# The second norm's mean from VectorE's accumulator, its variance from ScalarE's squares

## The chip, the core and the metric

The kernel runs on one core of a Trainium2 chip. Its engines are named as in the profile: PE is TensorE (matrix products), DVE VectorE, ACT ScalarE, POOL GpSimd, SP the engine that issues the DMA transfers. Each works through its own list of instructions in order and waits on semaphores for the others. The metric is the device time of one execution in microseconds (us); lower is better.

## The reference

```python
x = x + 0.5 * ffn(_layernorm(x, ...))       # x: 2048 tokens x 512
x = x + attn(_layernorm(x, ...))            # the "second norm" is this one
x = x + 0.5 * ffn(_layernorm(x, ...))

def _layernorm(x, axis=-1, eps=1e-05):
    m = jnp.mean(x, axis=axis, keepdims=True)
    v = jnp.var(x, axis=axis, keepdims=True)
    return (x - m) / jnp.sqrt(v + eps)

def ffn(x):     # 64 experts, each a bias vector; the best 8 of the softmax count
    scores = softmax(x @ router_weight.T + router_bias)
    topk_w, topk_idx = top_k(scores, 8)
    w_dense = zeros.at[..., topk_idx].add(topk_w)
    return x * topk_w.sum() + w_dense @ expert_bias

def attn(x):    # 32 heads of q, 8 of k and v, 128 wide, chunks of 128 tokens
    dt = softplus(x @ Win.T + dt_bias); g = -dt * exp(A_log)
    y = intra-chunk (scores * decay) @ (v * dt) + inter-chunk state
    return (rmsnorm(y) * gnorm_w * silu(x @ Wg.T)) @ Wo.T
```

## The kernel before

The 2048 tokens are 16 chunks of 128 tokens (one per partition), four chunks to a block; f counts blocks, 0 to 3 for the first ffn and 4 to 7 for the last. The order of every engine's instructions is written out by hand, and between engines there are only semaphores.

The run has three parts. A prologue of some 100 us does the first ffn, the second norm and what attention needs of its first block. Then 8 groups of heads x 16 steps follow, one chunk a step, and at the end the last ffn. Only the prologue has a second norm.

For each block the prologue goes as follows. The first norm's statistics come from DVE (`dve_stats` with w = 0) and POOL turns them into 1/sqrt(variance + eps), RSTD, and -mean times it, NMR (`pool_rstd`). PE turns the chunk (`pe_turn`), ACT copies it (`act_turned`, FXT), PE makes the logits, DVE adds the bias and finds the maxima (`dve_logits`, FLG), ACT takes the exponentials (`act_exp`, FEX), DVE weighs them (`dve_choose`, `dve_weigh`), PE turns the weights (`pe_weights`), ACT copies them (`act_weights`, FWT), PE mixes the experts' biases in two PSUM banks in turn (`pe_mix`), POOL scales the residual (`pool_residual`) and DVE adds the two in ACC (`dve_mixed`, L701). That is the experts' addition. Its result is what the second norm sees: `dve_stats` with w = 1 takes its statistics, `pool_rstd` again RSTD and NMR, ACT normalises into XN (`act_normalise`, L711), PE turns XN (`pe_turn2`, L720), ACT copies the high half as bf16 (`act_turned2`, XTH, L726) and DVE subtracts for the low half (`dve_turned2`, XTL, L733). PE's turns share three PSUM banks in rotation: turn k waits until turn k - 3 has been read, so the last turn of a block waits for XTL of its first chunk.

Woven in are weights (ACT makes WH, L1120, and POOL WL), the step sizes' softplus (`dve_dt_in`, ACT's Exp at L772, then `dve_series`, L779 to L801), and the first projections `fill`, whose banks ACT exchanges by halves for the rotary embedding (`swap`, QS, L1136 and L1137), POOL multiplies by the sine, and DVE multiplies by the cosine (`times_cos`, L1610) and adds (`add_sin`, L1615). `times_cos` of an item waits for its `swap`; a `swap` waits for the `add_sin` two items before. `gate` (L1161) is a Tanh of a projected bank.

## Time and profile before

| | |
|---|---|
| time, median of 3 runs | 1639.38 us (1639.04 to 1642.29) |
| profiled execution, its own time | 1642.75 us |
| its span | 1640.9 us |
| mean granted PE clock | 0.989 |
| busy share of the span | PE 97%, DVE 83%, ACT 67%, POOL 86% |

The span is what the profiler saw, from the first instruction to the last; the time holds 1.85 us more around it. The busy shares are means over the whole run. The row of 40 equal slices shows that the first three slices are unlike the rest: PE is at 7 to 9 tenths there, and at 9 in nearly all that follow.

### The profile page before, as it was taken

The page shows a single profiled execution, that of the slowest core. Times are in us where ns is not written, and L with a number is a line of the kernel's source. Part 1 is how long each engine was busy: PE and PEld are TensorE (multiplying, and loading weights), DVE is VectorE, ACT ScalarE, POOL GpSimd, SP SyncE. Part 2 cuts the span into 40 slices and gives each one's busy share as a digit, 9 for nine tenths or more (in the row PEclk, how much of TensorE's full clock was granted, in tenths as well). Part 3 has the DMA queues.
Part 4 walks back from the last instruction along what each step waited for, and adds up shares of the span by engine and source line. Part 5 has one row for each costly group of instructions (what it writes and reads, how often), then busy time and mean ns, then how long its engine had stood idle before and what let it go on. Part 6 is the DMA issues. An engine that isn't in the chain of part 4 may idle for free.

```text
span 1640.9 us, 33589 instructions
## 1 busy us (share of the span) xinstructions
PE 1589.4 (97%) x11028; PEld 883.8 (54%) x11028; DVE 1368.9 (83%) x2945; ACT 1093.0 (67%) x2987; POOL 1411.7 (86%) x1316
## 2 busy tenths in 40 slices
PE   7898999999999999999999999999999999999986
PEld 5554555555555555555555555555555555555554
DVE  6988788888878888787878888788888878788876
ACT  4666677676766677766766667666776667666653
POOL 4767899888988899888998989888998889888974
PEclk8999999999999999999999999999999999999998
DMA  5123233232333223231332224323342224322222
GB/s 211 39 55 67 55 74 87 65 72 52 78 85 78 53 59 102 54 83 47 91 78 64 61 64 92 72 72 53 73 95 59 72 46 97 72 65 52 53 45 103
DMA packets 208012, 118.76 MB, mean 72 GB/s; under 512 B 173792, under 2 KB 174816, under 8 KB 206816
## 3 DMA queue, kind: packets, MB, share of 16 engines
q1 hardware_dynamic: 207840, 116.63, 29.7%
q8 instruction: 89, 1.46, 0.4%
q14 instruction: 83, 0.68, 0.1%
HBM read 70.19 MB, written 4.46 MB: 45 GB/s over the span
## 4 chain that ended last, share of the span: by engine, by line
PE 74%; POOL 11%; DVE 8%; issue 4%; ACT 2%; DMA 0%; ACTq 0%; POOLq 0%; DVEq 0%
PE B L325 23%; PE B L323 23%; PE B L324 23%; POOL QS L1410 2%; POOL ROWS L1423 2%; POOL RR L1456 1%; DVE WL L1696 1%; POOL PL L1445 1%; PE B L553 1%; POOL ZS L1449 1%; POOL WVF L1433 1%; POOL K L1417 1%; POOL WVL L1441 1%; POOL RM L1453 1%; DVE PF L1640 1%
## 5 line engine op out<-in xcount | busy, mean ns | idle before, releaser
L323 PE MATMUL B<-WH,XTH 128*128 128x128 bf16 (+1 forms) x992 | 269.3, 296 | 0.6 <-DVE QF L1610 0.6
L324 PE MATMUL B<-WL,XTH 128*128 128x128 bf16 (+1 forms) x992 | 269.3, 296 | 0.0
L325 PE MATMUL B<-WH,XTL 128*128 128x128 bf16 (+1 forms) x992 | 269.3, 296 | 0.0
L1410 POOL TENSOR_TENSOR QS<-QS,SIN 128x512 f32<-128x512 f32 x160 | 219.3, 1371 | 42.8 <-ACT QS L1137 42.7
L323 PE MATMUL B<-XTH,WH 128*128 128x512 bf16 x640 | 243.2, 380 | 1.0 <-DVE G L1630 1.0
L325 PE MATMUL B<-XTH,WL 128*128 128x512 bf16 x640 | 243.3, 380 | 0.0
L324 PE MATMUL B<-XTL,WH 128*128 128x512 bf16 x640 | 243.2, 380 | 0.0
L1689 DVE SCALAR_TENSOR_TENSOR YF<-B,RR,G 128x128 f32<-128x128 f32 x512 | 144.2, 344 | 113.4 <-POOL RR L1456 113.3
L1169 ACT ACTIVATE PF<-ROWS,NG 128x128 f32<-128x128 f32 x512 | 162.7, 389 | 79.1 <-POOL ROWS L1423 78.8
L1449 POOL TENSOR_TENSOR ZS<-YF,ZS 128x512 bf16<-128x512 f32 x128 | 158.0, 1235 | 64.5 <-ACT ZS L1207 64.2
L1136 ACT ACTIVATE QS<-B 64x512 f32<-64x512 f32 x160 | 94.9, 593 | 150.3 <-PE B L325 143.5
L1423 POOL TENSOR_TENSOR ROWS<-ROWS,AFTER 128x512 f32<-128x512 f32 x128 | 189.8, 1483 | 2.4 <-DMA ROWS<-rows_dram 2.4
L323 PE MATMUL B<-WH,ZT 128*128 128x512 bf16 x480 | 181.9, 379 | 0.2 <-DVE ACC L1703 0.2
L324 PE MATMUL B<-WL,ZT 128*128 128x512 bf16 x480 | 181.9, 379 | 0.0
L325 PE MATMUL B<-WH,ZT 128*128 128x512 bf16 x480 | 181.9, 379 | 0.0
L1678 DVE TENSOR_TENSOR STL<-ST,STH 128x512 bf16<-128x512 f32 x120 | 145.1, 1209 | 39.4 <-ACT STH L1189 37.6
L1445 POOL TENSOR_TENSOR PL<-PF,PH 128x512 bf16<-128x512 f32 x128 | 148.1, 1157 | 17.8 <-ACT PH L1175 17.4
L1640 DVE SCALAR_TENSOR_TENSOR PF<-B,DT,PF 128x128 f32<-128x128 f32 x512 | 143.0, 339 | 21.7 <-ACT PF L1169 20.2
L1199 ACT ACTIVATE YF<-B 128x128 f32<-128x128 f32 x512 | 134.0, 276 | 31.1 <-DVE B L1656 28.2
L1615 DVE TENSOR_TENSOR QF<-QF,QS 128x512 f32<-128x512 f32 x128 | 138.0, 1080 | 5.1 <-POOL QS L1410 4.0
L1433 POOL TENSOR_TENSOR WVF<-VF,WJ 128x512 f32<-128x512 f32 x120 | 141.8, 1181 | 0.2
L1456 POOL TENSOR_TENSOR RR<-RM,HALF 128x4 f32<-128x4 f32 x128 | 132.8, 1037 | 10.0
(209 smaller groups left out, 4320.9 us busy)
## 6 DMA issues: line engine op xcount, KB each, us to landing
ROWS<-rows_dram SPq DMA_DIRECT2D x128, 256.0 KB, 3.2
STAGE<-in_wall SPq DMA_DIRECT2D x108, 256.0 KB, 2.8
ACC<-in_x SPq DMA_DIRECT2D x3, 1024.0 KB, 10.0
out<-ACC SPq DMA_DIRECT2D x3, 1024.0 KB, 3.9
ZT<-ZS SPq DMA_TRANSPOSE x128, 3.1
ACC<-in_x SPq DMA_DIRECT2D x4, 256.0 KB, 3.6
COS<-in_cos SPq DMA_DIRECT2D x1, 1024.0 KB, 12.0
SIN<-in_sin SPq DMA_DIRECT2D x1, 1024.0 KB, 14.7
```

The costliest lines, as they stand in the source:

```text
L323: nc.tensor.matmul(out_, ah, bh, start=first, stop=False)
L324: nc.tensor.matmul(out_, ah, bl, start=False, stop=False)
L325: return nc.tensor.matmul(out_, al, bh, start=False, stop=last)
L1169: ins = nc.scalar.activation(PF[:, c], ROWS[:, n % 2, c], ACT.Exp, bias=tab(NG, g, n)[:, h:h + 1], scale=-1.0)
L1410: nc.gpsimd.tensor_tensor(QS[:, sl, :], QS[:, sl, :], SIN[:, t0:t0 + TB], ALU.mult).then_inc(sin_ready.sem, 1)
L1423: nc.gpsimd.tensor_tensor(rows, rows, AFTER[:, None, :].broadcast_to([P, G, P]), ALU.add).then_inc(rows_masked.sem, 1)
L1433: nc.gpsimd.tensor_tensor(WVF[:, :, :], VF[b % 2][:, None, s * P:(s + 1) * P].broadcast_to([P, G, P]), tab(WJ, g, n)[:, :, None].broadcast ...
L1445: nc.gpsimd.tensor_tensor(PL[:, :], PF[:, :], PH[:, :], ALU.subtract).then_inc(pl_ready.sem, 1)
L1449: nc.gpsimd.tensor_tensor(ZS[:, 1, :], YF[:, :], ZS[:, 0, :], ALU.subtract).then_inc(zl_ready.sem, 1)
L1456: nc.gpsimd.tensor_tensor(RR[:, :], RM[:, :], HALF[:, :], ALU.pow).then_inc(rr_ready.sem, 1)
L1640: ins = nc.vector.scalar_tensor_tensor(PF[:, c], B_S[:, c], dt[:, h:h + 1], PF[:, c], ALU.mult, ALU.mult)
L1678: nc.vector.tensor_tensor(STL[:, :], ST[:, :], STH[:, :], ALU.subtract).then_inc(stl_ready.sem, 1)
```

## The change

The second norm takes its statistics in another way. DVE's experts' addition writes its sum over the 512 columns as well (`accum_out`, SM). POOL makes from it -mean/sqrt(512) (`pool_mean`, two chunks at a time). ACT squares the chunk with that as bias and 1/sqrt(512) as scale, and its accumulator sums the squares, which is the variance (`act_square`, VR); the squares themselves go to memory that is free at the time and aren't used. `pool_rstd` takes SM and VR in place of the aggregate. bn_stats and bn_aggr of the second norm are gone from DVE (16 and 16 of them).

```diff
-        def dve_stats(dve, w, f, chunks=range(BLK)):
+        def dve_stats(dve, f, chunks=range(BLK)):
...
+        def pool_mean(pool, f, half):
+            pool.wait_ge(f_acc.sem, f_acc.at(f, 2 * half + 1))
+            if f >= 2:
+                pool.wait_ge(f_sq.sem, f_sq.at(f - 2, BLK - 1))
+            c = slice(2 * half, 2 * half + 2)
+            nc.gpsimd.tensor_scalar(SMB[:, f % 2, c], SM[:, f % 2, c], -float(HID) ** -1.5, None, ALU.mult).then_inc(f_mean.sem, 1)
+
+        def act_square(act, f, chunks=range(BLK)):
+            A = chunks_of(f)
+            for i in chunks:
+                act.wait_ge(f_mean.sem, f_mean.at(f, i // 2))
+                if f >= 2:
+                    act.wait_ge(f_lg.sem, f_lg.at(f, 0))
+                    act.wait_ge(f_ve[1].sem, f_ve[1].at(f - 2, 0))
+                elif f:
+                    act.wait_ge(f_tp2.sem, f_tp2.at(f - 1, i))
+                nc.scalar.activation(XN[:, i, :] if f < 2 else FIRST.XT[:, f % 2, i, :], A[:, i, :], ACT.Square, bias=SMB[:, f % 2, i:i + 1],
+                                     scale=float(HID) ** -0.5, accum_out=VR[:, f % 2, i:i + 1]).then_inc(f_sq.sem, 1)
...
+            if w:
+                pool.wait_ge(f_sq.sem, f_sq.at(f, BLK - 1))
+            else:
+                pool.wait_ge(f_mv.sem, f_mv.at(f, 0))
...
+                if f < NB:
+                    if f >= 2:
+                        dve.wait_ge(f_nmr[1].sem, f_nmr[1].at(f - 2, 0))
+                    nc.vector.scalar_tensor_tensor(A[:, i, :], mix(f, i)[:, :], e.HRC[:, f % NB, i:i + 1], A[:, i, :],
+                                                   ALU.mult, ALU.add, accum_out=SM[:, f % 2, i:i + 1]).then_inc(f_acc.sem, 1)
+                    continue
...
+            act_square(act, 2, (0, 1))
             act_weights(act, 3)
             act_turned2(act, 1, (3,))
+            act_square(act, 2, (2, 3))
```

The squares of a block stand in two pairs on ACT, and `pool_mean` and `pool_rstd` on POOL before and behind them. Three places in the order of ACT, and one of DVE, matter below.

**First place.** ACT, block 1's squares between block 0's XTH and block 2's exponentials. Before:

```order
L1120 ACTIVATE WH<-WH 128x512 x2
L1239 ACTIVATE ALOG<-ALOG 128x32
L1120 ACTIVATE WH<-WL 128x512
L536 ACTIVATE FXT<-B 128x512
L1120 ACTIVATE WH<-WL 128x512
L536 ACTIVATE FXT<-B 128x512
L1120 ACTIVATE WH<-STAGE 128x512
L607 ACTIVATE FEX,FSUM<-FLG,FNM 128x64 x4
```

And now:

```order
L1153 ACTIVATE WH<-WH 128x512 x2
L1274 ACTIVATE ALOG<-ALOG 128x32
L1153 ACTIVATE WH<-WL 128x512
L486 ACTIVATE XN,VR<-ACC,SMB 128x512 x2
L562 ACTIVATE FXT<-B 128x512
L1153 ACTIVATE WH<-WL 128x512
L486 ACTIVATE XN,VR<-ACC,SMB 128x512 x2
L562 ACTIVATE FXT<-B 128x512
L1153 ACTIVATE WH<-STAGE 128x512
L633 ACTIVATE FEX,FSUM<-FLG,FNM 128x64 x4
```

Four squares (L486) have come ahead of the exponentials.

**Second place.** ACT around the weights' copy FWT of block 3, from the exchange of the second bank on. Before:

```order
L1137 ACTIVATE QS<-B 64x512
L726 ACTIVATE XTH<-B 128x4x128
L622 ACTIVATE FWT<-B 128x512
L726 ACTIVATE XTH<-B 128x4x128
L1136 ACTIVATE QS<-B 64x512
```

And now:

```order
L1170 ACTIVATE QS<-B 64x512
L759 ACTIVATE XTH<-B 128x4x128
L486 ACTIVATE FXT,VR<-ACC,SMB 128x512 x2
L648 ACTIVATE FWT<-B 128x512
L759 ACTIVATE XTH<-B 128x4x128
L486 ACTIVATE FXT,VR<-ACC,SMB 128x512 x2
L1169 ACTIVATE QS<-B 64x512
```

Block 2's squares stand before and behind FWT, ahead of the third exchange. On DVE, the same stretch, from the logits' end of block 3 to its weights; before:

```order
L572 TENSOR_SCALAR FNM<-FMX 128x4
L701 SCALAR_TENSOR_TENSOR ACC<-B,FHRC,ACC 128x512
L459 BN_STATS BS<-ACC 128x6
L578 MATCH_REPLACE FW<-FMX,FLG 128x64 x4
L581 TENSOR_TENSOR FW<-FLG,FW 128x256
L459 BN_STATS BS<-ACC 128x6
L464 BN_AGGR MV<-BS 128x2 x4
L588 TENSOR_TENSOR FW<-FW,FEX 128x256
```

And now:

```order
L598 TENSOR_SCALAR FNM<-FMX 128x4
L730 SCALAR_TENSOR_TENSOR ACC,SM<-B,FHRC,ACC 128x512
L604 MATCH_REPLACE FW<-FMX,FLG 128x64 x4
L607 TENSOR_TENSOR FW<-FLG,FW 128x256
L614 TENSOR_TENSOR FW<-FW,FEX 128x256
```

Two bn_stats and the aggregation have gone from between the addition and the weights.

**Third place.** ACT from dt's exponential (EG) to block 2's transposed copies. Before:

```order
L772 ACTIVATE EG<-EG 128x256
L1136 ACTIVATE QS<-B 64x512
L1137 ACTIVATE QS<-B 64x512
L711 ACTIVATE XN<-ACC,NMR,RSTD 128x512 x2
L1120 ACTIVATE WH<-STAGE 128x512
```

And now:

```order
L805 ACTIVATE EG<-EG 128x256
L1169 ACTIVATE QS<-B 64x512
L1170 ACTIVATE QS<-B 64x512
L486 ACTIVATE FXT,VR<-ACC,SMB 128x512 x2
L744 ACTIVATE XN<-ACC,NMR,RSTD 128x512 x2
L486 ACTIVATE FXT,VR<-ACC,SMB 128x512 x2
L1153 ACTIVATE WH<-STAGE 128x512
```

Block 3's four squares stand between the exponential and block 2's XTH.

## Rows read from the trace of the kernel before

**Rows 1.** Stretches (us from start): busy time of each engine, PE's granted clock.

```profile
core 0: us, PE busy (x) PEld busy (x) DVE busy (x) ACT busy (x) POOL busy (x), PEclk, DMA share, GB/s
28.00:101.00 73.00, 61.29 (x564) 40.83 (x564) 69.18 (x186) 50.57 (x114) 48.53 (x74) 0.98 0.16 38
29.50:33.10 3.60, 0.00 (x0) 0.00 (x0) 3.53 (x19) 3.15 (x11) 0.52 (x2) 0.96 0.00 0
33.10:36.40 3.30, 3.28 (x15) 2.03 (x16) 2.29 (x7) 2.81 (x6) 3.03 (x8) 0.53 0.01 2
...
78.90:82.00 3.10, 3.10 (x17) 1.68 (x18) 2.88 (x6) 2.46 (x6) 0.77 (x1) 1.00 0.31 85
...
100.90:104.30 3.40, 3.40 (x9) 1.16 (x8) 2.00 (x7) 1.38 (x5) 1.98 (x2) 0.52 0.14 33
...
100.76:1640.90 1540.14, 1506.02 (x10340) 826.02 (x10340) 1282.79 (x2705) 1032.37 (x2851) 1352.14 (x1214) 0.99 0.30 70
```

**Rows 2.** Groups by line on DVE, 20 to 80 us: busy us, mean ns, idle before.

```profile
L459 DVE BATCH_NORM_STATS2 BS<-ACC 128x6 f32<-128x512 f32 x24 | 15.6, 681 | 0.0
L701 DVE SCALAR_TENSOR_TENSOR ACC<-B,FHRC,ACC 128x512 f32<-128x512 f32 x16 | 11.8, 744 | 3.7 <-PE B L646 2.6 <-POOL ACC L670 0.9
```

**Rows 3.** Groups by line on ACT, the whole span: the activation tables' loads.

```profile
L536 ACT ACT_TABLE_LOAD x1 | 1.3, 1283 | 1.1 <-PEq L1934 1.1
```

**Rows 4.** ACT in order of time to 46 us: start, us, instruction, idle before.

```profile
26.04 0.60 ACT L536 ACTIVATE FXT<-B 128x512 f32<-128x512 f32 x1 [4.20 <-PE B L526]
...
39.60 1.14 ACT L1120 ACTIVATE WH<-WH 128x512 bf16<-128x512 f32 x2
...
44.89 0.35 ACT L607 ACTIVATE FEX<-FLG,FNM 128x64 f32<-128x64 f32 x1 [0.32 <-DVE FNM L572]
45.15 0.19 ACT L607 ACTIVATION_READ_ACCUMULATOR FEX<-FLG,FNM 128x1 f32 x1
45.24 0.33 ACT L607 ACTIVATE FEX<-FLG,FNM 128x64 f32<-128x64 f32 x1
```

**Rows 5.** ACT in order of time, 63 to 83 us.

```profile
63.07 0.60 ACT L622 ACTIVATE FWT<-B 128x512 bf16<-128x512 bf16 x1 [0.75 <-PE B L617]
...
64.18 0.59 ACT L1136 ACTIVATE QS<-B 64x512 f32<-64x512 f32 x1
...
70.16 0.59 ACT L1136 ACTIVATE QS<-B 64x512 f32<-64x512 f32 x1 [4.79 <-DVE QF L1615]
...
77.42 1.54 ACT L726 ACTIVATE XTH<-B 128x512 bf16<-128x512 f32 x3
...
82.68 2.92 ACT L711 ACTIVATE XN<-ACC,NMR,RSTD 128x512 f32<-128x512 f32 x4
```

**Rows 6.** DVE in order of time, 38 to 79 us.

```profile
38.87 1.28 DVE L459 BATCH_NORM_STATS2 BS<-ACC 128x6 f32<-128x512 f32 x2
...
43.16 0.85 DVE L564 SCALAR_TENSOR_TENSOR FLG<-B,RSTD,RB 128x64 f32<-128x64 f32 x4
...
45.49 0.38 DVE L464 BATCH_NORM_AGGREGATE MV<-BS 128x2 f32<-128x6 f32 x4
...
47.20 0.41 DVE L588 TENSOR_TENSOR FW<-FW,FEX 128x256 f32<-128x256 f32 x1
...
61.20 0.39 DVE L588 TENSOR_TENSOR FW<-FW,FEX 128x256 f32<-128x256 f32 x1
...
66.09 1.40 DVE L701 SCALAR_TENSOR_TENSOR ACC<-B,FHRC,ACC 128x512 f32<-128x512 f32 x2
...
74.26 1.19 DVE L779 TENSOR_SCALAR WJ<-EG 128x256 f32<-128x256 f32 x1
...
78.17 1.88 DVE L733 TENSOR_TENSOR XTL<-B,XTH 128x512 bf16<-128x512 f32 x3
```

**Rows 7.** PE in order of time: start, us, instruction, idle before.

```profile
41.97 1.00 PE L553 MATMUL B<-RWT,FXT 128*128 128x64 f32 x8
...
78.90 0.66 PE L720 MATMUL B<-IDF,XN 128*128 128x128 f32 x4 [1.84 <-DVE XTL L733]
...
100.76 0.39 PE L323 MATMUL B<-XTH,WH 128*128 128x512 bf16 x1 [1.05 <-DVE G L1630]
```

**Rows 8.** POOL in order of time.

```profile
24.63 0.20 POOL L479 TENSOR_TENSOR NMR<-NMR,RSTD 128x4 f32<-128x4 f32 x1
```

More of the change, by code:

```diff
@@ L157, in build @@
         CONST = sb("CONST", [P, 4 * P])
-        BS = sb("BS", [P, 2, 2, BLK, 6])
-        MV = sb("MV", [P, 2, 2, BLK, 2])
+        BS = sb("BS", [P, 2, BLK, 6])
+        MV = sb("MV", [P, 2, BLK, 2])
+        SM, SMB, VR = (sb(n, [P, 2, BLK]) for n in ("SM", "SMB", "VR"))
         VE = sb("VE", [P, 2, 2, BLK])
@@ L282, in build @@
         w_landed = [Sem(f"w_landed{i}") for i in range(2)]
-        f_mv, f_ve, f_rstd, f_nmr = ([Sem(f"{n}{w}", 1) for w in range(2)] for n in ("f_mv", "f_ve", "f_rstd", "f_nmr"))
-        f_bs = [Sem(f"f_bs{w}", 4) for w in range(2)]
+        f_mv = Sem("f_mv", 1)
+        f_ve, f_rstd, f_nmr = ([Sem(f"{n}{w}", 1) for w in range(2)] for n in ("f_ve", "f_rstd", "f_nmr"))
+        f_bs = Sem("f_bs", 4)
+        f_mean, f_sq = Sem("f_mean", 2), Sem("f_sq", 4)
         f_xn = Sem("f_xn", 4)
@@ L443, in chunks_of @@
             return ACC[:, f % NB * BLK:(f % NB + 1) * BLK, :]
-        def dve_stats(dve, w, f, chunks=range(BLK)):
-            if w == 0 and 0 < f < NB:
+        def dve_stats(dve, f, chunks=range(BLK)):
+            if 0 < f < NB:
                 dve.wait_ge(x_landed[f].sem, 16)
             if f >= 2:
-                dve.wait_ge(f_nmr[w].sem, f_nmr[w].at(f - 2, 0))
+                dve.wait_ge(f_nmr[0].sem, f_nmr[0].at(f - 2, 0))
             A = chunks_of(f)
             for i in chunks:
-                if w == 0 and f == 0:
+                if f == 0:
@@ L454, in dve_stats @@
                     dve.wait_ge(x0_landed[i].sem, 16)
-                if w == 1:
-                    dve.wait_ge(f_acc.sem, f_acc.at(f, i))
                 if f >= NB:
                     dve.wait_ge(out_free.sem, out_free.at(KVH - 1, (f - NB) * BLK + i))
-                nc.vector.bn_stats(BS[:, w, f % 2, i, :], A[:, i, :]).then_inc(f_bs[w].sem, 1)
+                nc.vector.bn_stats(BS[:, f % 2, i, :], A[:, i, :]).then_inc(f_bs.sem, 1)
             if BLK - 1 not in chunks:
                 return
-            dve.wait_ge(f_bs[w].sem, f_bs[w].at(f, BLK - 1))
+            dve.wait_ge(f_bs.sem, f_bs.at(f, BLK - 1))
@@ L463, in dve_stats @@
             for i in range(BLK):
-                ins = nc.vector.bn_aggr(MV[:, w, f % 2, i, :], BS[:, w, f % 2, i, :])
-            ins.then_inc(f_mv[w].sem, 1)
+                ins = nc.vector.bn_aggr(MV[:, f % 2, i, :], BS[:, f % 2, i, :])
+            ins.then_inc(f_mv.sem, 1)
+        def pool_mean(pool, f, half):
[4 more added lines that the diff above has]
+            nc.gpsimd.tensor_scalar(SMB[:, f % 2, c], SM[:, f % 2, c], -float(HID) ** -1.5, None, ALU.mult).then_inc(f_mean.sem, 1)
@@ L473, in pool_rstd @@
                 pool.wait_ge(f_l.sem, f_l.at(f - 2, 0))
-            nc.gpsimd.tensor_tensor(VE[:, w, f % 2, :], MV[:, w, f % 2, :, 1], EPSC[:, :], ALU.add)
-            nc.gpsimd.tensor_scalar(NMR[:, w, f % 2, :], MV[:, w, f % 2, :, 0], -1.0, None, ALU.mult).then_inc(f_ve[w].sem, 1)
+            mean, var, to_mean = (SM[:, f % 2, :], VR[:, f % 2, :], 1.0 / HID) if w else (MV[:, f % 2, :, 0], MV[:, f % 2, :, 1], 1.0)
+            nc.gpsimd.tensor_tensor(VE[:, w, f % 2, :], var, EPSC[:, :], ALU.add)
+            nc.gpsimd.tensor_scalar(NMR[:, w, f % 2, :], mean, -to_mean, None, ALU.mult).then_inc(f_ve[w].sem, 1)
             pool.wait_ge(f_ve[w].sem, f_ve[w].at(f, 0))
@@ L1476, in _ @@
             pool_rstd(pool, 0, 1)
+            pool_mean(pool, 0, 0)
+            pool_mean(pool, 0, 1)
             pool_rstd(pool, 1, 0)
@@ L1494, in _ @@
             split_lo(0, 5)
+            pool_mean(pool, 2, 0)
+            pool_mean(pool, 2, 1)
             pool_scales(pool, 3)
@@ L1499, in _ @@
             pool_rstd(pool, 1, 2)
+            pool_mean(pool, 3, 0)
             split_lo(0, 8)
+            pool_mean(pool, 3, 1)
             split_lo(0, 7)
```

47 lines of the change are left out of this document (22 added, 25 removed).

## The prediction

> **What bounds the kernel now.** I read the view of stretches first [rows 1], then who holds what in them: from 28 to 101 us DVE is busy for 69.2 of 73.0 us, PE for 61.3, POOL for 48.5 and ACT for 50.6. Nearly everything that the edit touches lies there; behind 100.76 us only work stands that it leaves alone, PE busy for 1506 of 1540 us. So what the change can move is the stretch in which PE isn't yet the bound. It is worth what it moves the instant at which PE begins the step loop (the multiplication at 100.76 us, which waited for DVE) [rows 7], and I take it that the rest follows one for one. What then matters is not how busy DVE is but which wait ends last at each hand-over between ACT, DVE and PE, and I walked through them in order of time.
>
> **What is removed.** 16 bn_stats of the second norm, of 681 ns each [rows 2]. Those that stand one behind the other start 0.60 us apart (two take 1.28 us, one 0.68 [rows 2, 6]), so they hold DVE for 16 x 0.60 = 9.6 us; 16 bn_aggr in four groups, 0.38 us a group [rows 6], about 0.3 us of which delays the next, give 1.2 us. DVE gets 10.8 us back. That is the most the change could give.
>
> **What is added to ACT.** 16 Squares over 128x512 with a bias that lies in SBUF, an immediate scale and an accumulator output. The nearest rows: a copy from SBUF without pointers, 0.52 us from start to start (two in 1.14 us, the last of them 0.62) [rows 4]; the normalisation with two pointers, 0.71 (four in 2.92, the last one 0.80) [rows 5], so a pointer costs about 0.095; the accumulator's read-out delays the next instruction by 0.09 (45.15 to 45.24 us) [rows 4]. That makes 0.52 + 0.095 + 0.09 = 0.70 us a Square, 11.3 us in all. Its bounds are 0.61 (the pointer free) and 0.80 (as dear as two). Activation tables add nothing: there is one load in the whole run [rows 3], though Exp, Tanh, Identity and Square alternate.
>
> **What is added to DVE and POOL.** No row shows a DVE accumulator. From below it costs nothing; from above, an addition takes twice its 744 ns [rows 2]. ACT's read-out at 0.09 is the nearest row, and 0.1 is what I take; only two or four additions stand where it counts, 0.2 to 0.4 us. The eight small products on POOL are like its other 128x4 work (0.2 us a piece [rows 8]); POOL is idle for a third of the stretch, and they hide in that. Were they not hidden they would cost 8 x 0.2 = 1.6 us. The Squares of a block now stand between the addition and the variance, but the old statistics did so too.
>
> **Step 1, to 47 us: DVE's time comes back to it as idleness.** The Squares of block 0 fit into the 4.2 us for which ACT stood idle before 26.04 [rows 4] (POOL can give the mean behind its product at 24.63 [rows 8], at 25.1) and delay the copy at 26.04 by 0.5, which PE needs at 27.2: nothing is lost. In block 1, DVE loses three bn_stats ahead of block 2's logits, but PE itself finishes these at 42.97 us [rows 7], where DVE came at 43.16 [rows 6]: 1.8 us removed give 0.2. On ACT four Squares (2.8 us) now stand ahead of block 2's Exp (first place in the order). From 39.60 us it had five copies to do, a short Exp (0.12) and two copies from PSUM (0.50 each), 3.7 us of work in 5.3, so 1.6 us idle [rows 4]. Exp of block 2 starts not at 44.89 but at 39.60 + 3.7 + 2.8 = 46.1. Its four pieces follow at 0.33 us (45.24 is the read-out's end and the second piece's start), so it ends near 47.55 instead of 46.3. DVE weighs at 47.20 [rows 6]; it now waits until 47.57. **+0.4 us**, although DVE lost a statistic and an aggregation (1.0 us) there.
>
> **Step 2, to 62 us: a gain.** Carried on, block 3's logits start at 55.9 instead of 55.78 (PE's own pace, plus 0.4). Behind them DVE loses two statistics and an aggregation (1.6 us) before it weighs block 3: 59.7 instead of 61.20 us. That is **-1.5 us** on DVE. It is the only place at which the removal reaches a hand-over in full.
>
> **Step 3, to 74 us: ACT takes it back.** ACT reaches the weights' copy of block 3 at 63.07 us, having waited for PE [rows 5]. Now two Squares stand before it and two behind it, ahead of the exchange of halves at 64.18 (second place) [rows 5]. From 61.9 us on: copy 0.50, Squares 1.40, weights at 63.8, copy, Squares to 66.2, exchange 66.2 to 67.4 instead of 64.18 to 65.4. DVE's multiplication by the cosine waits for that exchange, so the additions of block 3 start at 68.0 instead of 66.09 [rows 6]: **+1.9**. Two statistics fewer behind them leave +0.7, and ACT's next exchange, which waits for DVE, starts at 70.8 instead of 70.16 [rows 5]. That exchange (1.2 us), the normalisation of two chunks (0.71 each), a copy (0.52) and dt's Exp follow without a gap; DVE's series, which waits for the last, begins at 74.4 instead of 74.26 [rows 6]: **+0.1**.
>
> **Step 4, to 83 us: the decisive one.** From there ACT had no gap of more than 0.1 us, and four Squares stand ahead of the first transposed copy of block 2 (third place) [rows 5]: 77.42 + 0.12 + 4 x 0.70 = 80.3 us. DVE, which had reached its counterpart at 78.17 [rows 6], is there no later than before, and idles from 78.3 to 81.0. Its subtraction there ran at 78.17 and now runs at 81.0. This is **+2.8 us** with the 0.1 in it, and the same for PE, whose last turn of block 2 waited for DVE at 78.90 [rows 7]. DVE, ACT and PE are then all 2.8 late, in the same order as before and with no idle time to make it up until 95 us.
>
> **Step 5: PE's clock.** PE now pauses from 78.2 to 81.7 us behind a first pause of 1.5. Where it had paused from 29.5 to 33.1 us [rows 1] the granted clock behind it was 0.53, the 1.2 GHz level, for 3.3 us; after the wait that ends at 100.76, 0.52 for 3.4 us [rows 1]. The wait of 1.84 us before 78.90 [rows 7] left it at 1.00 [rows 1]. After 3.5 us it more likely falls, and a stretch at half speed as long as those two loses 1.7 us on PE. The gate's Tanh waits for that multiplication and the normalisation of block 3 for the Tanh, so about 1.1 us of it reaches DVE. I weigh it at 0.7: **+0.8 us**.
>
> **Sum.** 2.8 + 0.8 = **+3.6 us**. Of the profiled execution (1642.75 us, span 1640.9, 1.85 around it) it makes 1646.3; that execution lies 3.4 us above the median of the runs, and against the median of 1639.38 it makes 1643.0. With Squares at 0.61 us step 3 ends at -0.5 and step 4 adds 2.4, so +1.9 without a fall of the clock; at 0.80 it is +4.0, and 5.1 with one.
>
> **Rivals.**
> (a) *DVE really is the bound, and its 10.8 us come through in part* (faster). For it: DVE's 95% in the stretch, and that the chain of waits runs over DVE for most of it. Against it: steps 1 and 4. It needs ACT to get through the Squares in idle time; the point from which it decides is ACT reaching block 2's transposed copies at 77.4 us or before. That takes dt's Exp at 71.5 instead of 74; if step 2's 1.5 us survive and a Square costs little, it is -1.5 to -6 us: 1633 to 1638. Chance 0.12.
> (b) *The Squares are cheap or partly absorbed* (no change that can be measured): ACT's lateness meets slack that I haven't seen, behind 86 us or in the first steps. 0 to +3.2 us, 1639.4 to 1642.6, 1641 in the middle. Chance 0.33, which holds the lower part of my own sum.
> (c) *My sum*, +3.3 to +4.8. Chance 0.43.
> (d) *An addition with the accumulator runs at half rate*, the upper bound from above: +0.6 us for each of 16, of which two stand before the exchange at 70.16 and one or two before block 3's logits, so +1.2 to 1.9 on top of my sum, 1644.2 to 1644.9. For it: no row shows such an instruction; against it: an addition reads one source from PSUM and one from SBUF. With it goes that in-order ACT holds up something that I haven't seen (+5 to +8). Chance 0.12. The Trainium skill, "Vector Engine (DVE) Microarchitecture Reference", "Points that are easy to get wrong", says that the scalar_tensor_tensor form with two sources in SBUF that aren't bf16 runs at half throughput, since no read port is left for the accumulator. By that rule, if it held for this mixed case too, the sum would be the one just given; no run so far shows it.
>
> **How the numbers follow.** The likeliest is (c), 1643.0 us. A measurement here tells 0.2% (3.3 us, so 1642.7) from no change, and my forecast stands almost on that line. Slower by more: 0.40 of (c) and 0.11 of (d), 0.51. Within 0.2%: (b), 0.03 of (c), 0.02 of (a) and 0.01 of (d), 0.39. Faster: 0.10, the rest of (a), which takes its gains above 3.3 us. The range leaves out 0.1 at the bottom, most of (a), and under 0.1 at the top: 1637.5 to 1646.5.
>
> **What would show it.** Step 1: Exp of block 2 on ACT at about 46.1 us and DVE waiting for ACT before it weighs. Step 2: block 3's weights on DVE at 59.7. Step 3: DVE's second cosine product waits for ACT's exchange. Step 4: an idle DVE of about 2.7 us before the subtraction XTL of block 2, put down to ACT, near 78 us, and a Square that costs 0.70 from start to start. Step 5: a granted clock near 0.5 right behind 81.7 us. PE's step loop then begins at 104 to 105 us instead of 100.76. The prediction is wrong if DVE isn't idle at 78 us, if a Square costs 0.6 or 0.8, or if the start of the loop is later and the end isn't.

## The result and the profile after

The changed kernel takes 1646.45 us (median of 6 runs, 1645.16 to 1650.19), the kernel before, over the 6 runs beside them, 1641.67. The ratio of the two is 1.0034, 95% interval 1.0024 to 1.0044: about 0.3% slower, 4 to 7 us. A second set of 12 runs gave 1646.44 and a ratio of 1.0026 (1.0016 to 1.0036). The profiled execution took 1645.60 us, span 1643.8. It is 2.9 us longer than the profiled one of before (1642.75), less than the medians differ: its prologue is 5.1 us longer, its loop 2.2 us shorter (1537.94 against 1540.14 [rows 1]); the experiments come back to the loop.

Stretches of the changed kernel (busy time of PE, PEld, DVE, ACT, POOL, then the granted clock, the DMA share and GB/s), to be read beside [rows 1]:

```profile
28.00:101.00 73.00, 60.26 (x549) 40.29 (x548) 57.92 (x165) 55.82 (x130) 46.11 (x77) 0.93 0.12 31
78.40:81.70 3.30, 0.17 (x3) 0.01 (x1) 0.76 (x2) 3.30 (x9) 1.55 (x4) 0.76 0.00 0
81.70:85.00 3.30, 3.30 (x10) 1.74 (x11) 2.62 (x6) 2.33 (x6) 1.19 (x2) 0.50 0.28 82
85.00:88.40 3.40, 3.40 (x12) 1.33 (x11) 3.19 (x9) 1.31 (x3) 0.00 (x0) 0.71 0.00 0
105.86:1643.80 1537.94, 1503.87 (x10340) 825.43 (x10340) 1283.32 (x2705) 1033.21 (x2851) 1352.89 (x1214) 0.99 0.30 70
```

DVE has lost 11.3 us of its 69.2 in the first stretch and ACT gained 5.2, so the work moved as it should (a part of each now lies behind 101 us); but PE does nearly nothing from 78.4 to 81.7, and behind that it runs at 0.50 of its clock and then 0.71 (before: 1.00).

The new instructions, as groups of the stretch from 20 to 106 us (busy time, mean ns of one, idle time before them):

```profile
L486 ACT ACTIVATE XN<-ACC,SMB 128x512 f32<-128x512 f32 x8 | 5.7, 712 | 3.4 <-POOL SMB L474 3.4
L486 ACT ACTIVATION_READ_ACCUMULATOR XN<-ACC,SMB 128x1 f32 x8 | 1.5, 190 | 0.0
L730 DVE SCALAR_TENSOR_TENSOR ACC<-B,FHRC,ACC 128x512 f32<-128x512 f32 x15 | 11.0, 746 | 4.6 <-PE B L672 3.5 <-POOL ACC L696 0.9
L730 DVE DVE_READ_ACCUMULATOR ACC<-B,FHRC,ACC 128x1 f32 x15 | 1.2, 82 | 0.0
L474 POOL TENSOR_SCALAR SMB<-SM 128x2 f32<-128x2 f32 x8 | 2.2, 269 | 2.8 <-DVE ACC L730 2.3
```

The first two lines are the Squares of blocks 0 and 1, which write to XN; the eight of blocks 2 and 3 write to FXT and last the same. A Square lasts 712 ns and its read-out 190, but they overlap: the next instruction starts 0.70 us behind the Square (79.11 to 79.81 below). The addition on DVE is as long as it was in [rows 2] (746 against 744 ns).

ACT by time (start, duration, what, and in brackets the idle time before it and who ended it), beside [rows 4] and [rows 5]:

```profile
45.73 0.34 ACT L633 ACTIVATE FEX<-FLG,FNM 128x64 f32<-128x64 f32 x1
63.64 0.58 ACT L648 ACTIVATE FWT<-B 128x512 bf16<-128x512 bf16 x1
66.13 0.59 ACT L1169 ACTIVATE QS<-B 64x512 f32<-64x512 f32 x1
79.11 0.71 ACT L486 ACTIVATE FXT<-ACC,SMB 128x512 f32<-128x512 f32 x1
79.81 0.61 ACT L1153 ACTIVATE WH<-STAGE 128x512 bf16<-128x512 f32 x1
80.33 1.54 ACT L759 ACTIVATE XTH<-B 128x512 bf16<-128x512 f32 x3
87.54 0.60 ACT L1194 ACTIVATE G<-B 128x512 f32<-128x512 f32 x1 [2.09 <-PE B L920]
```

The gate in the last line (G) had no wait before:

```profile
82.18 0.60 ACT L1161 ACTIVATE G<-B 128x512 f32<-128x512 f32 x1
```

DVE, beside [rows 6]; then PE, beside [rows 7]:

```profile
42.65 0.86 DVE L590 SCALAR_TENSOR_TENSOR FLG<-B,RSTD,RB 128x64 f32<-128x64 f32 x4 [1.53 <-PE B L579]
47.19 0.43 DVE L614 TENSOR_TENSOR FW<-FW,FEX 128x256 f32<-128x256 f32 x1 [1.40 <-ACT FEX L633]
59.80 0.42 DVE L614 TENSOR_TENSOR FW<-FW,FEX 128x256 f32<-128x256 f32 x1
67.36 0.69 DVE L1659 TENSOR_TENSOR QF<-B,COS 128x512 f32<-128x512 f32 x1 [1.33 <-ACT QS L1170]
74.35 1.18 DVE L812 TENSOR_SCALAR WJ<-EG 128x256 f32<-128x256 f32 x1 [1.15 <-ACT EG L805]
80.94 1.89 DVE L766 TENSOR_TENSOR XTL<-B,XTH 128x512 bf16<-128x512 f32 x3 [2.62 <-ACT XTH L759]
```

```profile
81.69 1.11 PE L753 MATMUL B<-IDF,XN 128*128 128x128 f32 x4 [3.12 <-DVE XTL L766]
82.60 0.63 PE L915 MATMUL B<-WH,XTH 128*128 128x512 bf16 x1
105.86 0.39 PE L326 MATMUL B<-XTH,WH 128*128 128x512 bf16 x1 [1.05 <-DVE G L1679]
```

Read in order: XTL of block 2 waits 2.62 us for ACT's XTH, PE's last turn of block 2 waits 3.12 for XTL, and the fill behind it (`fill` number 6, the sixth below) starts at 82.60. Its products last 0.63 us instead of 0.38, so the gate on ACT waits another 2.09 for PE. PE begins the loop at 105.86 instead of 100.76 us [rows 7].

### The profile page after: what moved, and what is told of

It is laid out like the page before. It is cut to its first block, busy times and chain, and to the rows that moved or that the text cites. A ratio compares the mean times of both kernels' runs of the same rounds, so it can differ in the third digit from the quotient of the medians.

```text
span 1643.8 us, 33637 instructions
## 1 busy us (share of the span) xinstructions
PE 1589.2 (97%) x11028; PEld 883.8 (54%) x11028; DVE 1359.7 (83%) x2929; ACT 1104.8 (67%) x3019; POOL 1414.5 (86%) x1324
## 4 chain that ended last, share of the span: by engine, by line
PE 75%; POOL 11%; DVE 6%; issue 4%; ACT 3%; DMA 1%; ACTq 0%; POOLq 0%; DVEq 0%
PE B L326 23%; PE B L328 23%; PE B L327 23%; POOL ROWS L1464 2%; POOL QS L1451 2%; POOL RR L1497 1%; PE B L579 1%; POOL PL L1486 1%; DVE WL L1745 1%; DMA STAGE<-in_wall 1%; POOL ZS L1490 1%; POOL WVF L1474 1%; POOL K L1458 1%; POOL WVL L1482 1%; POOL RM L1494 1%
## 5 line engine op out<-in xcount | busy, mean ns | idle before, releaser
L1232 ACT ACTIVATE YF<-B 128x128 f32<-128x128 f32 x512 | 134.5, 277 | 31.7 <-DVE B L1705 28.7
```

## The experiments

All kernels below differ from the changed one or the one before by the edit shown. One measure needs a word ahead. The first 43 us spread from execution to execution: block 2's logits stand on DVE at 43.16 us in the profile before [rows 6], and at 40.55 and 41.08 in two kernels that do the same work up to there (before_loop_filled; sum_only, with its accumulators); from 20 to 26 us PE ran at 0.50 of its clock in the first and at 0.9 to 1.00 in the other two. So I count the **stretch** from block 2's logits on DVE to the loop's first product on PE. It was 57.60 us before (100.76 - 43.16), 57.63 and 57.59 in the two others, and 63.21 in the changed kernel (105.86 - 42.65). What the change does ahead of the logits is left out of it; the prediction puts that at 0.2 us, and the spread hides it. The stretch has two parts, which meet where DVE starts XTL of block 2: up to there the order of the work decides (35.01 us from the logits before, 38.29 changed), behind it PE's clock (22.5 to 22.7 us in every kernel whose clock held or fell earlier, 23.9 to 24.9 where it fell there; squares_later's 29.3 have another reason).

| kernel | logits | loop | stretch | logits to XTL | PE's pause, clock behind it | median, us | ratio (95%) |
|---|---|---|---|---|---|---|---|
| before | 43.16 | 100.76 | 57.60 | 35.0 | 1.84, kept | 1641.7 | |
| changed | 42.65 | 105.86 | 63.21 | 38.3 | 3.12, fell for 6.8 | 1646.45 | 1.0034 (1.0024 to 1.0044) |
| after_again | 43.44 | 106.54 | 63.10 | 38.3 | 3.12, fell for 6.8 | 1646.44 | 1.0026 (1.0016 to 1.0036) |
| squares_added | 43.27 | 107.11 | 63.84 | 39.2 | 3.12, fell for 3.4 | 1648.05 | 1.0039 (1.0025 to 1.0052) |
| stats_gone | 40.49 | 97.34 | 56.85 | 32.9 | 1.86, fell for 3.4 | 1638.64 | 0.9983 (0.9974 to 0.9992) |
| pe_kept_busy | 43.59 | 104.57 | 60.98 | 38.3 | filled, kept | 1644.48 | 1.0018 (1.0009 to 1.0027) |
| block3_dve | 43.01 | 104.49 | 61.48 | 38.9 | 0.54, fell earlier for 3.4 | 1646.48 | 1.0031 (1.0021 to 1.0041) |
| behind_swap | 42.64 | 98.86 | 56.22 | 33.8 | 1.49, kept | 1640.02 | 1.0000 (0.9989 to 1.0011) |
| behind_swap_all_act | 43.16 | 103.96 | 60.80 | 36.9 | 3.12, fell for 3.4 | 1646.35 | 1.0027 (1.0016 to 1.0038) |
| squares_later | 43.96 | 108.11 | 64.15 | 34.8 | 2.54, fell for 6.8 | 1648.96 | 1.0039 (1.0027 to 1.0052) |
| all_act_filled | 42.85 | 102.27 | 59.42 | 36.9 | filled, kept | 1642.93 | 1.0003 (0.9994 to 1.0011) |
| behind_swap_filled | 43.54 | 99.80 | 56.26 | 33.7 | filled, kept | 1639.77 | 0.9988 (0.9980 to 0.9996) |
| sum_only | 41.08 | 98.67 | 57.59 | 35.1 | 1.84, kept | 1641.83 | 1.0003 (0.9994 to 1.0012) |
| before_loop_filled | 40.55 | 98.18 | 57.63 | 35.1 | 1.84, kept | 1641.77 | 1.0009 (1.0000 to 1.0018) |

The pause is the one ahead of block 2's last turn on PE; "fell for 6.8" says that the granted clock then stood at 0.50 for 6.8 us. The ratio goes by the mean of the runs. The times of the logits, of XTL and of the loop come from one profile a kernel.

**squares_added.** DVE's second statistics come back where they were (their results are used), ScalarE's squares stay where the change put them (unread).

```
             dve_mixed(dve, 3, (0, 1))
+            dve_stats1(dve, 3, (0,))      # bn_stats as before; likewise blocks 0 to 2
             dve_dt_in(dve, 1)
```

> The changed kernel with VectorE's second statistics put back where they stood before: GpSimd takes mean and variance from them again, while ScalarE's 16 squares and GpSimd's 8 means still run at the change's places, their results unread (the normalisation still waits for the squares). Theory (the squares stand in ScalarE's order ahead of what VectorE waits for, and what VectorE is relieved of is worth about 1 us of the start, since it waits there for others): the trigonometric series of the pair of blocks 2 and 3, at 74.35 us in the changed kernel and 74.26 before, comes at about 76.0, the XTL of block 2 (80.94) at about 82.1, the first product of the main loop (105.86) at 106.5 to 107.2, so 1 us over the changed kernel, 6 us over the kernel before. Rival (VectorE's relief was worth nearly all its 10.8 us, and hid a larger cost of the squares): the loop starts at 110 or later, 10 us or more over the kernel before.

The loop starts at 107.11 us, the stretch is 0.6 longer than the changed kernel's and 6.2 longer than before, the median 1.6 above the changed kernel's. In this kernel nothing is taken from DVE, and the whole loss is there and a little more: it comes from the squares on ACT. DVE's relief is worth 0.9 us up to XTL and 0.6 of the stretch, of the 10.8 us that it amounts to. DVE waits as in the changed kernel (its timeline):

```profile
82.45 1.89 DVE L788 TENSOR_TENSOR XTL<-B,XTH 128x512 bf16<-128x512 f32 x3 [2.59 <-ACT XTH L781]
```

**stats_gone.** The reverse: no squares and no means; the variance of the second norm is left out (a constant 1).

```
-            act_square(act, 2, (0, 1))    # and the seven other pairs
-            pool_mean(pool, 2, 0)         # and the seven others
+            nc.gpsimd.memset(VR[:, :, :], 1.0)
```

> The changed kernel without the 16 squares on ScalarE and the 8 means on GpSimd; the variance is left out (a constant 1 stands for it), the mean is still the sum of VectorE's accumulator. It shows what VectorE's relief is worth alone. Theory (VectorE waits for ScalarE and TensorE at several places of the start, so that only what lies between the waits arrives): the weighing of block 3 at about 58.4 us (61.20 before), the series at about 70.7 (74.26), the XTL of block 2 at about 74.6, the main loop's first product at about 97.2, 3.5 us ahead of the kernel before. Rival (VectorE is the bound of the start, all of its 24 instructions of 681 ns less their readouts arrive): the loop's first product at 91 to 93, 8 to 10 us ahead of before. Second rival (no gain, since TensorE and DMA set the pace): 100 to 101.

The loop's first product is at 97.34, as expected, but by luck: 2.7 us of that were gained ahead of 43 us. Counted from the logits, XTL of block 2 is 2.2 us earlier than before (73.35 - 40.49 = 32.9 against 35.0), and the loop 0.8. So even with nothing put on ACT the 10.8 us are worth 2.2, and 1.4 of these were lost to the clock: behind a pause of 1.86 us it fell, where behind 1.84 it had stayed in three profiles of the kernel before and its likes. PE by time, and the stretch around it:

```profile
74.08 0.66 PE L752 MATMUL B<-IDF,XN 128*128 128x128 f32 x4 [1.86 <-DVE XTL L765]
```

```profile
74.00:77.50 3.50, 3.37 (x11) 1.56 (x13) 3.25 (x8) 2.74 (x6) 0.85 (x1) 0.62 0.25 75
```

(The "24 instructions" of the rival above are the bn_stats of both norms in [rows 2]; 16 of them are gone.) The measured gain is 2.8 us (1.3 to 4.3), more than the stretch says. The rest must lie ahead of 43 us or in the loop; one profile doesn't tell.

**pe_kept_busy.** Work without use in PE's pause.

```
-            pe_turn2(pe, 2)
+            pe_turn2(pe, 2, (0, 1, 2))
+            pe.wait_ge(f_acc.sem, f_acc.at(3, 3))
+            for _ in range(14):
+                nc.tensor.matmul(BANK[5][:, :], WH[:, 0, 0:P], WH[:, 0, :], start=True, stop=True)
+            pe_turn2(pe, 2, (3,))
```

> The changed kernel with 14 more 128x512 products into an unused bank, put on TensorE between the third and the last chunk of block 2's turns, where it waits 3.12 us for VectorE (78.57 to 81.69 us). Nothing reads them. Theory (of the 5.1 us that the loop starts later, 2.8 are the squares behind which XTH and XTL of block 2 stand, and 2.3 are TensorE's clock, granted at 0.76, 0.50 and 0.71 in the three slices after that wait): the granted clock stays near 1.00 from 78 to 88, the last turn of block 2 still begins near 81.7, the gate that waits for the sixth fill (87.54) comes at 85.2 to 85.6, the loop's first product at 103.4 to 104 instead of 105.86, the kernel about 2 us faster than the changed one. Rival (what follows 81.7 is set by ScalarE and VectorE, the low clock lies beside their work): the clock is up but the loop still starts at 105.5 to 106, or later if the products themselves are in the way.

Two stretches behind the pause, and PE at the loop's start:

```profile
81.70:85.00 3.30, 3.20 (x17) 1.56 (x16) 2.94 (x5) 2.79 (x7) 2.05 (x3) 1.00 0.07 12
85.00:88.40 3.40, 3.40 (x21) 1.57 (x19) 3.19 (x10) 3.40 (x6) 0.00 (x0) 1.00 0.21 68
```

```profile
104.57 0.39 PE L326 MATMUL B<-XTH,WH 128*128 128x512 bf16 x1 [1.05 <-DVE G L1683]
```

The clock stays at 1.00 from the pause on, ACT doesn't wait for the sixth fill (3.40 of 3.40 us busy where it was 1.31), and the stretch shrinks from 63.2 to 61.0. That is 2.2 us for the clock alone (XTL comes 38.29 us behind the logits, exactly as in the changed kernel), and the median falls by 2.0. In this profile the clock did fall once earlier, from 65.5 to 69 us; XTL shows no delay from it. The loop stands at 104.57 only because this execution reached its logits 0.9 us later.

**block3_dve.** Block 3's statistics back on DVE; no squares, means or accumulator for it.

```
-            act_square(act, 3, (0, 1))    # and (2, 3)
-            pool_mean(pool, 3, 0)         # and 1
+            dve_stats1(dve, 3, (2, 3))    # and (0,), (1,) at their old places
```

> The changed kernel with block 3's second statistics as they were before (VectorE's statistics at their old places, none of ScalarE's squares nor GpSimd's means for block 3, and no accumulator in its additions); blocks 0 to 2 as changed. Theory (the 2.8 us between the series at 74.35 and the XTL of block 2 at 80.94 are block 3's four squares, which stand ahead of XTH of block 2 on ScalarE): the series comes at about 75.7 (two statistics now lie on VectorE ahead of it), the XTL of block 2 at about 79.6, the loop's first product at 102.2 if the clock stays up and 104.4 if it falls; so 1.5 to 3.6 us faster than the changed kernel and still 1.5 us or more behind the one before, the rest being block 2's squares. Rival (all of the loss comes from block 3's squares): the loop's first product at 100.8 or earlier, as before.

The loop is at 104.49, where I expected it with a fallen clock, but on another way. The series came at 77.81, 2 us later than expected. DVE's two additions of the sine products (`add_sin`; the expectation above calls them products) and the instruction ahead of them now meet POOL's low parts of the weights (DVE by time, then POOL):

```profile
71.05 1.16 DVE L824 SCALAR_TENSOR_TENSOR EG<-DT 128x256 f32<-128x256 f32 x1
72.13 2.24 DVE L1683 TENSOR_TENSOR QF<-QF,QS 128x512 f32<-128x512 f32 x2
```

```profile
70.77 2.45 POOL L1465 TENSOR_TENSOR WL<-STAGE,WH 128x512 bf16<-128x512 f32 x2
```

In squares_added, with the same statistics on DVE but POOL later, the same three took 0.41 and 1.29 us. PE, which waited 3.35 us for the last QF, had its fall of the clock at 77 to 80.5 instead of 80 to 87. So this edit removes one delay and makes another: XTL is 38.9 us behind the logits. The stretch is 1.7 us shorter than the changed kernel's, since no low clock follows XTL, and yet the median is the same; see the end of the next section.

**behind_swap.** block3_dve, and block 2's four squares moved on ACT:

```
-            act_square(act, 2, (0, 1))
             act_weights(act, 3)
             act_turned2(act, 1, (3,))
-            act_square(act, 2, (2, 3))
             swap(0, 0, 2, 2)
+            act_square(act, 2, (0, 1))
+            act_square(act, 2, (2, 3))
             swap(0, 0, 3, 3)
```

> Block 3's second statistics on VectorE as in block3_dve, and block 2's four squares, which stood ahead of ScalarE's exchange of halves of the third item, put behind it. Theory (1.9 of the lost time arises there, because VectorE's cosine product waits for that exchange): the exchange begins at about 63.3 us instead of 66.5 in block3_dve, VectorE doesn't wait 1.33 for it, the trigonometric series comes at 73.0 to 74.3 (77.8 in block3_dve), the XTL of block 2 at 76.9 to 78.2, and the loop's first product at 99.5 to 101, so between 1.2 us ahead of the kernel before and level with it, 3 to 5 us faster than block3_dve. Rival (VectorE's order and not the exchange sets it, or GpSimd's products beside VectorE's slow it again as in block3_dve, where two products of the sine took 2.24 us instead of 1.28): the series at 76 or later, the loop at 102.5 or later.

ACT by time, then DVE:

```profile
63.33 0.59 ACT L1192 ACTIVATE QS<-B 64x512 f32<-64x512 f32 x1
68.98 0.59 ACT L1192 ACTIVATE QS<-B 64x512 f32<-64x512 f32 x1 [1.50 <-DVE QF L1683]
```

```profile
72.93 0.75 DVE L835 TENSOR_SCALAR WJ<-EG 128x256 f32<-128x256 f32 x1
76.39 1.87 DVE L789 TENSOR_TENSOR XTL<-B,XTH 128x512 bf16<-128x512 f32 x3
```

The exchange is at 63.33 us and the four squares lie in a gap (ACT still waits 1.50 us behind them). The stretch is 56.22, 5.3 us shorter than block3_dve, just beyond the 3 to 5 that I expected: the move takes away step 3's delay, the meeting with POOL and the fall of the clock together. Three of eleven executions took 1645.7 us, so the median is 1.4 below before and the mean equal to it.

**behind_swap_all_act.** The changed kernel with that move alone.

> The changed kernel with one move alone: block 2's four squares behind ScalarE's exchange of the third item instead of two each ahead of it, all squares still on ScalarE. Theory: the exchange at about 63.3 instead of 66.1, the series at 72.3 to 72.6 (74.35 in the changed kernel), but block 3's four squares still stand ahead of XTH of block 2, which comes at about 78.3 (80.33), the XTL at about 78.9; the loop's first product at 101.5 if TensorE's clock holds and 103.7 if it falls in the pause ahead of that XTL; 2 to 4 us faster than the changed kernel and level with the one before or up to 3 us behind. Rival (the 1.9 us of that place were hidden behind something else, and only the later squares count): no more than 0.5 us faster than the changed kernel.

DVE by time:

```profile
73.48 0.85 DVE L812 TENSOR_SCALAR WJ<-EG 128x256 f32<-128x256 f32 x1 [1.65 <-ACT EG L805]
80.06 1.89 DVE L766 TENSOR_TENSOR XTL<-B,XTH 128x512 bf16<-128x512 f32 x3 [2.55 <-ACT XTH L759]
```

Counted from the logits, the series is 1.4 us earlier than in the changed kernel (30.3 against 31.7), XTL of block 2 still waits 2.55 us for the four squares of block 3, and XTL, too, is 1.4 us earlier (36.9 against 38.3). Both delays are thus where the prediction has them. The stretch is 2.4 us shorter, because 1.0 more comes from the clock, which stood at 0.50 for 3.4 us here and for 6.8 in the changed kernel. Yet the median is 1646.35. In its profile the clock fell at the loop's start too (0.66, 0.50 and 0.70 in the slices from 104 to 108.5 us), as in that of before, which the changed kernel's two profiles don't show.

**before_loop_filled.** The kernel before with work in the pauses just ahead of the loop.

```
             pe_rows(pe, 1)
+            for _ in range(3):
+                nc.tensor.matmul(BANK[5][:, :], WH[:, 0, 0:P], WH[:, 0, :], start=True, stop=True)
...
                     scores(g, n + 1)
+                if g == 0 and n == 0:
+                    for _ in range(4):
+                        nc.tensor.matmul(BANK[5][:, :], WH[:, 0, 0:P], WH[:, 0, :], start=True, stop=True)
```

> The kernel before with seven more 128x512 products into an unused bank, three ahead of the scores at 98.89 us, where TensorE waits 0.80, and four ahead of the loop's first fill at 100.76, where it waits 1.05. Nothing reads them. In the profiled executions the loop took 1540.1 us (before) and 1540.0 (block3_dve) where the clock was granted at 0.5 in its first 3.4 us, and 1537.9 to 1538.7 where it was 1.00 (changed kernel, pe_kept_busy, stats_gone). Theory (this fall comes in some executions and not in others, hangs on the pause of about 2 us just ahead of the loop, and costs 2 us): the clock stays at 1.00 behind 100.8, the loop still begins at 100.8 to 101.0, the profiled execution and the median are at 1639 to 1640.5, 1.5 to 2.7 us below the kernel before. Rival (the fall hangs on something else or the runs differ by something else): the median within 0.7 us of the kernel before.

PE at the loop's start:

```profile
98.18 0.39 PE L323 MATMUL B<-XTH,WH 128*128 128x512 bf16 x1 [0.19 <-DVE G L1635]
```

The pause is filled and the clock at 1.00 behind it, but the median is 1641.77: the rival holds. From the loop's first product to the end the profiled execution took 1540.5 us, no less than before; the clock fell near 1576 us instead. squares_added had already spoken against the theory: its clock was at 1.00 at the loop's start and its loop took 1540.4 us. What separates long loops from short ones is how many times the clock falls in them. Ahead of the last 10 us of the run it fell four times in the seven profiles whose loop took 1540.0 to 1540.5 us (before, squares_added, block3_dve, behind_swap_all_act, behind_swap_filled, sum_only and this one) and three times in the seven with 1537.8 to 1538.7; the fourth fall lay at the loop's start in some and near 1576 to 1586 us in others. So one more fall goes with some 2 us, and filling one pause has not removed it here.

**sum_only.** The accumulator alone, in the kernel before, on its 16 additions of the first ffn.

```
+                                               ALU.mult, ALU.add, accum_out=SM[:, f, i:i + 1]).then_inc(f_acc.sem, 1)
```

> The kernel before with the accumulator output on its 16 additions and nothing else changed; the sums are not read. Theory (a read-out of 82 ns behind each addition, of which 0.01 to 0.02 us delays the next instruction): the addition takes 0.74 to 0.75 us as before, the series stands at 74.3 to 74.5, the median within 0.5 us of the kernel before. Rival (the accumulator takes 0.1 us or more from VectorE each time): the series 0.4 us or more later and the median 0.5 to 1 us above it.

The two groups of the addition on DVE:

```profile
L703 DVE SCALAR_TENSOR_TENSOR ACC<-B,FHRC,ACC 128x512 f32<-128x512 f32 x16 | 11.7, 743 | 1.9 <-PE B L647 0.9 <-POOL ACC L671 0.9
L703 DVE DVE_READ_ACCUMULATOR ACC<-B,FHRC,ACC 128x1 f32 x16 | 1.3, 81 | 0.0
```

The stretch is 57.59 and the median 1641.83, ratio 1.0003: the accumulator costs nothing that can be measured. (The series stood at 72.29, not 74.3: again the early part of the execution. From the logits it is 31.2 against 31.1.)

**after_again.** The changed kernel, unchanged.

> The changed kernel once more, unchanged. The executions profiled so far differ ahead of 43 us by up to 2.6 us for the same program (block 2's logits on VectorE at 43.16 us in the kernel before, at 40.55 and 41.08 in two kernels that are the same up to there), and in the loop by 2 us with where the clock falls. Counted from block 2's logits to the loop's first product, the kernel before took 57.60, 57.59 and 57.63 us, the changed kernel 63.21. Theory (that stretch is the same in every execution of a program, the rest is spread): 63.0 to 63.4 again, though the loop's first product itself may stand 2 us earlier or later, and the median at 1646 to 1647. Rival (the 63.21 was chance, as the early part is): a stretch that differs by 1 us or more.

The stretch is 63.10. It repeats within 0.1 us, as it does for the kernel before, while the logits moved by 0.8.

**all_act_filled.** behind_swap_all_act with the 14 products of pe_kept_busy and the 7 of before_loop_filled.

> behind_swap_all_act with TensorE kept at work in its pauses: 14 products ahead of block 2's last turn as in pe_kept_busy, and 3 and 4 ahead of the loop as in before_loop_filled. behind_swap_all_act moved block 2's squares only, took 60.80 us from block 2's logits to the loop (63.21 in the changed kernel) and still had the changed kernel's median, with a fall of the clock at 104 to 108 us that the changed kernel's profile does not have. Theory (the two savings add up: 2.4 for the order, 1.0 to 2.2 for the clock at 80 us, and the loop's fall is avoided): 58.6 to 59.8 us from the logits to the loop, clock at 1.00 from 75 us on, a median of 1642.5 to 1644. Rival (what the clock loses in one place it loses in another when that is filled, as in before_loop_filled): the stretch as said but a median of 1644.5 or more.

A stretch of 59.42 and a median of 1642.93, both within what was expected: with all squares on ACT, better placed and the clock held, the kernel is level with the one before (ratio 1.0003), not faster.

**behind_swap_filled.** behind_swap with six products in PE's pause and the 7 ahead of the loop.

> behind_swap (block 3's second statistics on VectorE, block 2's squares behind the exchange) with six products ahead of block 2's last turn and 3 and 4 ahead of the loop. behind_swap took 56.22 us from block 2's logits to the loop, 1.4 less than the kernel before, and its median was 1.4 us lower (1640.02 against 1641.45), with three of eleven executions at 1645.7. Theory (those three are falls of the clock in the pause of 1.49 us ahead of block 2's last turn): none of them at 1645, the stretch at 56.1 to 56.4, the median at 1639.5 to 1640.5. Rival (the pauses have no part in them): one or more executions at 1645 again, or a median above 1641.

No execution above 1641.9, a median of 1639.77, ratio 0.9988 (0.9980 to 0.9996). It is the only version with the whole computation that beats both kernels, by 0.12%, the price being 13 products whose results nobody reads. That behind_swap's three executions at 1645.7 were falls of the clock is in keeping with it, not shown: they have no profile, and of the 29 executions of the kernel before that ran beside this kernel two also took 1646.6 and 1647.95 us.

**squares_later.** All squares on ACT, block 2's behind the exchange, block 3's behind the transposed copies of block 2 (shown; the move of block 2's is that of behind_swap).

```
-            act_square(act, 3, (0, 1))
             act_normalise(act, 2, (2, 3))
-            act_square(act, 3, (2, 3))
             split_hi(0, 9)
             act_turned2(act, 2)
+            act_square(act, 3)
```

> The changed kernel with all squares still on ScalarE, block 2's four behind the exchange of the third item (as in behind_swap_all_act) and block 3's four behind the transposed copies XTH of block 2 instead of ahead of them. Theory (the loss is where the squares stand, not that ScalarE has 11.3 us more to do): VectorE doesn't wait 2.6 us for XTH, TensorE's pause there is 1.9 or less and the clock stays up; ScalarE's next work (the gate that stood at 82.18 us before) comes up to 2.8 us later less the 1.2 gained ahead of it, and the stretch from block 2's logits to the loop takes 58.5 to 59.3 us (57.6 before, 63.2 changed); the median 1642.5 to 1644. Rival (ScalarE has no slack behind 80 us either, and GpSimd's chain from the squares to the normalisation of block 3 comes on top): 60.5 us or more, as behind_swap_all_act.

It is the slowest of all, and for a reason that neither theory had. DVE's wait for XTH shrinks to 0.58 us as meant, and XTL is back at 34.8 us from the logits (35.0 before, 36.9 with block 2's squares moved alone, 38.3 changed). PE's pause doesn't shrink with it (2.54 us), because the turns ahead of it also came earlier (they end 33.0 us from the logits, 35.9 in the changed kernel), and the clock fell. But POOL stands in its order at the norm's reciprocal root, which waits for block 3's squares, and behind it stands a weight's low part that PE's sixth fill needs (POOL by time, then PE):

```profile
84.16 0.20 POOL L500 TENSOR_TENSOR VE<-VR,EPSC 128x4 f32<-128x4 f32 x1 [6.78 <-ACT FXT L486]
86.49 1.15 POOL L1443 TENSOR_TENSOR WL<-STAGE,WH 128x512 bf16<-128x512 f32 x1
```

```profile
87.69 0.39 PE L920 MATMUL B<-WL,XTH 128*128 128x512 bf16 x1 [2.37 <-POOL WL L1443]
```

POOL idles for 6.78 us, PE for 2.37 in the middle of a fill, and its clock falls twice (78.8 to 85.6, 89 to 92.5 us). The squares were moved past ACT's queue, but not past POOL's.

## Why the prediction was off in size

The forecast was 1643.0 us and the measurement 1646.45, 3.45 above it and at the very top of the range of 1637.5 to 1646.5. The direction and the chain of waits were right; one term of the sum was too small, and so was the base.

**What held.** The frame held: who ends which wait decided, not DVE's share of busy time. A Square costs 0.70 us from start to start (79.11 to 79.81), as worked out. Step 1: Exp of block 2 at 45.73 (46.1 said), DVE waits for it. Step 2: weights of block 3 at 59.80 (59.7). Step 3: the exchange at 66.13 (66.2), DVE's cosine product waits for it, the series at 74.35 (74.4). Step 4: XTH at 80.33 (80.3), DVE's wait of 2.62 and its subtraction at 80.94 (81.0). That these times agree to some 0.1 us is partly luck: this execution reached its logits 0.5 us before the profile of the kernel before, and after_again, which is the same program, has them all 0.8 us later. Counted from the logits, step 2 gives 0.9 us and not 1.5, and XTL is 3.3 us late and not 2.8. behind_swap_all_act and squares_later show whose delays these are: moving block 2's squares takes XTL from 38.3 to 36.9, moving block 3's as well to 34.8, where it was before. The chance was highest on slower by over 0.2%, and it is slower by 0.3%.

**The step that failed is step 5**, "I weigh it at 0.7: +0.8 us". The mechanism was right and its size too small by a factor of nearly three. The clock did fall, so the weight of 0.7 goes. It stood low not for 3.4 us behind the first product but for 6.8, from 80.1 us, ahead of it, to 86.9: the fill took from 82.60 to 87.3 at 0.43 us a product where it had run at 0.22. And the loss on PE reached the gate in full: ACT waited 2.09 us for it, where I had taken 1.1 of 1.7. Both errors count. In squares_added and stats_gone the clock was low for just the 3.4 us that I had assumed; ACT waited 1.67 us, and the way from XTL to the loop was 2.1 and 1.4 us longer than before (1.3 in behind_swap_all_act), more than 1.1 already. In the changed kernel it was 2.3 longer. pe_kept_busy prices the whole at 2.2 us. With 2.2 in place of 0.8 the sum is 2.8 + 2.2 = 5.0, and the loop's start moved by 5.1 (105.86 - 100.76). It came at 105.86, outside the 104 to 105 that I had named. Counted from the logits it is 3.3 for the order (XTL of block 2 at 80.94 - 42.65 = 38.3 against 35.0) and 2.3 for the clock.

**The base.** 1643.0 was 1639.38 + 3.6, and 1639.38 was the median of three runs, of which two were near the bottom of the spread. In three later sets of 24, 29 and 29 runs the kernel before has medians of 1641.92, 1641.45 and 1641.73. Beside the changed kernel it was 1641.67, 2.3 us above the base, and that is most of the distance of 3.45 between forecast and measurement; the other 1.2 goes with what step 5 lacked (1.4). By the medians the change costs 4.8 us, by the stretch 5.6.

**The smaller terms.** I put 0.1 us on DVE's accumulator; it is 0.01 to 0.02 from start to start, and rival (d), an addition at half rate, is refuted by sum_only. The rule of the Trainium skill cited there ("Vector Engine (DVE) Microarchitecture Reference", "Points that are easy to get wrong") speaks of two sources in SBUF; for one in PSUM and one in SBUF this case shows 743 ns with the accumulator and 744 without. Rival (a) made the change up to 6 us faster by DVE's relief; squares_added prices that relief at 0.6 us of the stretch, and stats_gone, with nothing put on ACT, at 2.2 us up to XTL. Rival (b), slack behind 86 us, is not there: the delay of 4.8 us at XTL of block 3 (92.44 against 87.64) is still 5.1 at the loop.

**What stays open.** behind_swap_all_act and block3_dve have stretches 2.4 and 1.7 us shorter than the changed kernel's and its median. In their profiles the clock fell four times in the loop and not three times, which took 2.6 and 2.1 us (1540.54 and 1540.01 against 1537.94) and would explain it; but these are single profiles, and whether it holds for the executions without one isn't shown. By the same token "the rest follows one for one" of the prediction holds roughly for the medians (5.6 us of stretch, 4.8 measured), and did not for the two profiled executions. Why the clock falls in the loop where it does, the profiles don't tell.

## What to carry to other kernels

Work taken from an engine that waits for others buys little: 10.8 us off DVE were worth 0.6 to 2.2. Work given to an engine that is half idle costs where it stands, in program order, ahead of a hand-over: of the 2.8 us of block 3's Squares 2.1 arrived at XTL, of block 2's 1.4. Look for the gap first, and at the orders of all engines that wait for the result, POOL's too (squares_later). And when a delay opens a pause on TensorE, price the clock with it, at every product up to where it is seen to recover; to compare single profiles, count from an event just ahead of the edit, not from the start.
